# Splitting a second layer's weights in every second step of the first layer, over 16 steps

## The reference

```python
x = x + attention_1(layernorm(x), ctx)     # one head of 512, context of 8 x 120 rows, softmax(q k^T) v
x = x + int8_product(layernorm(x), rhs)    # rows and columns scaled to +-127, rounded, multiplied, scaled back
x = x + attention_2(layernorm(x), ctx)     # 16 heads of 32, weights w_q, w_k, w_v, w_o
x = x + experts(layernorm(x))              # 8 routed experts with capacity 640, one shared expert
```

## Time and profile before

| | before |
|---|---|
| median of the runs | 1309.65 us (1308.88 to 1310.9) |
| the profiled execution | 1312.34 us |
| its span, first to last instruction | 1310.6 us |
| busy in the span: PE, VectorE (DVE), ScalarE (ACT), GpSimd (POOL) | 1238.8, 784.9, 681.1, 574.5 us |
| mean granted TensorE clock | 0.984 |

### The profile page before, as it was taken

One profiled execution on the slowest core, in us unless ns is written; L12 is line 12 of the kernel. 1 busy time (PEld: TensorE's weight loads), 2 busy tenths in 40 slices (PEclk: granted clock), 3 DMA queues, 4 the chain that ended last, 5 costly groups with the idle time before them and its releaser, 6 DMA issues. The chain is left out here.

```text
span 1310.6 us, 27659 instructions
## 1 busy us (share of the span) xinstructions
PE 1238.8 (95%) x10196; PEld 777.5 (59%) x10196; DVE 784.9 (60%) x1615; ACT 681.1 (52%) x1931; POOL 574.5 (44%) x685
## 2 busy tenths in 40 slices
PE   6889998799999999996999999999999999999994
PEld 3556665588888888873444444444444444666762
DVE  5899898799999999893766612121212132544440
ACT  4377777799999999882442111111111121555551
POOL 0056667655666566643000377775002000356533
PEclk9999998999999999998999999999999999899998
DMA  9511023134344434437410402030207000688835
GB/s 347 186 65 66 2 31 44 50 110 142 114 138 138 138 120 134 135 111 161 26 33 1 97 1 65 2 65 2 65 1 241 1 33 9 203 166 221 165 50 71
DMA packets 115445, 122.90 MB, mean 94 GB/s; under 512 B 52816, under 2 KB 77552, under 8 KB 115312
## 3 DMA queue, kind: packets, MB, share of 16 engines
q1 hardware_dynamic: 97472, 98.67, 25.8%
q0 software_dynamic: 13248, 21.15, 8.7%
q10 hardware_dynamic: 4592, 1.32, 0.5%
HBM read 72.35 MB, written 48.80 MB: 92 GB/s over the span
## 5 line engine op out<-in xcount | busy, mean ns | idle before, releaser
L1921 DVE SCALAR_TENSOR_TENSOR shared_hf<-shared_ps_u,shared_sg 128x512 f32<-128x512 f32 x64 | 44.2, 691 | 275.1 <-PE shared_ps_u L111 260.7
L1648 POOL DMA_INDIRECT lists<-shared_load,shared_index x128 | 126.6, 989 | 166.9 <-DVE shared_sk L1789 125.5
L1322 ACT ACTIVATE att_early<-bank,att_early 128x120 f32<-128x120 f32 x512 | 178.9, 377 | 14.1 <-DVE att_early L1190 14.0
L111 PE MATMUL shared_ps_g<-program_xs,program_wgu 128*128 128x512 f16 x768 | 178.4, 382 | 3.5 <-PEq L103 3.5
L1960 PE MATMUL shared_ps_y<-shared_wd,shared_hid 128*128 128x512 f16 x768 | 176.1, 379 | 1.7 <-DVE program_res L1947 1.7
L111 PE MATMUL shared_ps_u<-program_xs,program_wgu 128*128 128x512 f16 x768 | 176.2, 379 | 0.0
L1890 ACT ACTIVATE shared_sg<-shared_ps_g 128x512 f32<-128x512 f32 x64 | 38.2, 597 | 215.3 <-PE shared_ps_g L111 215.3
L1810 POOL DMA_INDIRECT program_x<-xn_rows,program_ex_slots x40 | 38.5, 963 | 243.6 <-PE experts_ps_x L2172 148.4
L111 PEld LDWEIGHTS shared_ps_g<-program_xs,program_wgu 128*128 128x128 f16 x768 | 75.6, 99 | 95.3 <-issue 6.3
L1960 PEld LDWEIGHTS shared_ps_y<-shared_wd,shared_hid 128*128 128x128 f16 x768 | 75.1, 98 | 92.6 <-DVE program_res L1947 2.2
L111 PEld LDWEIGHTS shared_ps_u<-program_xs,program_wgu 128*128 128x128 f16 x768 | 75.1, 98 | 90.7 <-issue 0.2
(11 more groups left out here) (292 smaller groups left out, 2465.5 us busy)
## 6 DMA issues: line engine op xcount, KB each, us to landing
att_place<-q_rows SPq DMA_DIRECT2D x96, 128.0 KB, 2.6
xn_rows<-att_late SPq DMA_DIRECT2D x37, 256.0 KB, 3.1
q_rows<-att_early SPq DMA_DIRECT2D x32, 256.0 KB, 2.1
xt_tiles<-att_late SPq DMA_DIRECT2D x32, 256.0 KB, 2.0
out_rows<-program_res SPq DMA_DIRECT2D x32, 256.0 KB
program_xs<-xt_tiles SPq DMA_DIRECT2D x28, 256.0 KB, 5.1
program_x<-in_x SPq DMA_DIRECT2D x6, 1024.0 KB, 5.4
att_qr<-in_sh_guT SPq DMA_DIRECT2D x8, 512.0 KB, 4.6
```

Source lines behind the costliest of these rows:

```text
L111: last = pe.matmul(out, lhs(a, k), rhs(b, k), start=n == 0, stop=n == len(terms) - 1)
L1322: last = act.activation(prob[:, c, h, :], ps_s[c % 2][:, h, :], ACT.Exp, bias=nmax[:, u % 2, c, h:h + 1], accum_out=rsum[:, u % 2, n:n + 1])
L1648: pool.indirect_dma_start(out=io["lists"], out_offset=bass.IndirectOffsetOnAxis(ap=index[:, t, k:k + 1], axis=0), in_=load[:, t, k, :], in ...
L1921: dve.scalar_tensor_tensor(hf[:, c % 2], ps_u[c % 2][:, :], HS / WS, sg[:, c % 2], ALU.mult, ALU.mult).then_inc(s["hf"], 1)
```

## The change

Before, the eight calls of `split` follow one another in eight steps: ScalarE's in steps 2 to 9, VectorE's in steps 3 to 10. After, there is one in every second step: ScalarE's in steps 2, 4, ... 16, VectorE's in steps 3, 5, ... 17. The order of the weights, the calls themselves and every wait stay.

```diff
     SPLITS = ["L0_Wv", "L1_wvT", "L1_wkT", "L1_wqT", "L1_woT"]
+
+    SPLIT_AT = {2: ("L1_wvT", 0), 4: ("L1_wvT", 1), 6: ("L1_wkT", 0), 8: ("L1_wkT", 1),
+                10: ("L1_wqT", 0), 12: ("L1_wqT", 1), 14: ("L1_woT", 0), 16: ("L1_woT", 1)}
...
             if t == -5:
                 for k in range(KC):
                     quantised(k)
-            if 2 <= t < 10:
-                split(("L1_wvT", "L1_wkT", "L1_wqT", "L1_woT")[(t - 2) // 2], t % 2)
+            if t in SPLIT_AT:
+                split(*SPLIT_AT[t])
...
             if t == -2:
                 columns_out()
-            if 3 <= t < 11:
-                split(("L1_wvT", "L1_wkT", "L1_wqT", "L1_woT")[(t - 3) // 2], (t + 1) % 2)
+            if t - 1 in SPLIT_AT:
+                split(*SPLIT_AT[t - 1])
```

## The result

The changed kernel takes 1315.74 us (median of 19 runs, 1312.0 to 1319.37). The kernel before, run beside it, takes 1311.25 us (19 runs, 1308.31 to 1316.34); the three runs shown first had a median of 1309.65. The ratio is 1.0024, with a 95% interval of 1.0012 to 1.0035: slower by about 3.1 us, between 1.6 and 4.6. (The two medians lie 4.5 us apart, near the upper end of that interval.) The profiled span went from 1310.6 to 1314.5, by 3.9.

The account below looks back on a forecast made before the run. VectorE was taken to set the pace of the front layers until step 11, PE from there. A gain of 3.1 us in steps 4 to 10 and a cost of 5.4 in steps 11 to 17 gave +2.2, 1311.9 us; range 1308.3 to 1313.6.

Parts of the forecast that it names:

- O(18): Start of step 18's weighted-sum matmuls on PE, from which a step is counted; forecast 2.2 us later than before.
- Step 8 goes to 5.73 if VectorE allows: Step 8, losing its VectorE split, falls to PE's 5.73 us, with L685 in the split's place; gain 1.12.
- Step 10 (6.89) likewise: Step 10, also without its VectorE split, falls from 6.89 to 5.73 us; gain 1.16.
- slower: Rival: VectorE still last in steps 8 and 10 through L685 behind L437; up to 2.3 us, 1314.2; chance 0.17.
- so step 11 is priced like 13: Step 11: step 10's ScalarE split falls behind L506, so it takes 7.07 instead of 5.73 us, 1.34 lost.
- Steps 4 to 7: First region: step 4's change gains 0.28 us, step 6 gains 0.57, step 7 keeps its split and about 6.86.
- The odd steps 13, 15, 17: Second region: late ScalarE split and VectorE's split waiting for L437 make each 7.07 instead of 5.73 us; 1.34 lost.
- the bound that I gave for a split that gets in first: Odd late steps: if VectorE's split starts before L437, PE follows at 6.19 us, loss 0.46 a step.
- The even steps 12 to 16: Second region, steps without a VectorE split: 1.05 us of VectorE idle time, nothing further lost or recovered, 5.73 each.
- SyncE's reloads: Four reloads of x, after steps 5, 9, 13, 17, each first read four steps later; cost nothing.
- Shorter stalls: Rival: split beats L437 (forecast to lose by 0.28) or costs a flat 1.56 us; 1308.3 to 1310.1; chance 0.17.
- Faster: Rival: VectorE's 1.05 us idle time and PE's distance to L731 hide the late splits whole; 1306.5; chance 0.06.

Follow-up runs that it names:

- e2: Changed kernel with ScalarE's high part of the v0 jobs in steps 7 to 10 moved ahead of `integers`; 1468.96 us, one run (kernel before 1468.88, other chip).
- e1: Changed kernel with only VectorE's splits spread, ScalarE's back in steps 2 to 9; 1471.02 us, one run (kernel before 1468.88, other chip).
- e3: Changed kernel with GpSimd's second residual cut to one column for tiles 5, 7, 9, 11; 1466.27 us, one run (kernel before 1468.88, other chip).
- e6: Changed kernel with the late splits moved to idle places inside the same steps; 0.9999 of the kernel before (0.9983 to 1.0015).
- e4: Control: kernel before with the same early ScalarE high part as e2; 1470.97 us, one run (kernel before 1468.88, other chip).
- e5: Changed kernel with the edits of e1 and e2 together; 0.9995 of the kernel before (0.9981 to 1.0008).
- e7: wvT and wkT splits as before, wqT and woT one per step in e6's places, plus e2's early high part; 0.9979 of the kernel before (0.9965 to 0.9992).

## Why the prediction was right or wrong

**The time.** Forecast: 1311.9, +2.2, no change that could be told. Measured: +3.1 by the ratio, 1315.74 by the median, above the range's 1313.6. Of the 3.8 us between 1311.9 and 1315.74, 1.6 are the reference itself (1311.25 in the longer series against 1309.65), 1.1 are the step below, as O(18) shows, and 1.1 are not located: the medians lie 4.5 us apart where the traces' first layers lose 3.3. The step below alone would have given 1313.0, inside the range. The side was the forecast's, toward slower; its size went past the 0.2% mark (2.6 us): 2.2 us lie under it, the traces' 3.3 above.

**The step that failed: "Step 8 goes to 5.73 if VectorE allows ... gain 1.12. Step 10 (6.89) likewise: gain 1.16."** Measured gains: 0.14 and 0.13. I let L685 take the split's place at O + 4.36 and asked only whether GpSimd would be in its way. Its input from ScalarE, which comes at O + 5.73, I didn't look up; in the trace of before that wait didn't show because the split stood in front of it. e2 shows it: with that one instruction earlier, the two steps take 5.73 and 5.78. The rival "slower" had the right place and the right price (VectorE still last in steps 8 and 10, up to 2.3 us; it was 2.0) but the wrong cause, the meeting with GpSimd, which e2 measures at what the sum had for it, with PE still last in step 8.

**Step 11: "so step 11 is priced like 13".** It lost 0.51, not 1.34, only because step 10 was still late: ScalarE found its job early and its split was hidden. In e2 the step takes 6.99. This is the same error's other side; together: 0.98 + 1.03 - 0.83 for steps 8, 10 and 11 and -0.09 for the others is +1.1, from the forecast's 2.2 to the measured 3.3. That the two sums lie so near owes something to luck: at O(11) the gain is 1.13 instead of 3.13, and the cost behind it 4.46 instead of 5.36; the first error brought the second with it, and the second cancels part of the first.

**What held.** Steps 4 to 7 (O(6) earlier by 0.27 and O(7) by 0.84; VectorE's freed time in step 4 went to a wait of 0.81 at 78.95 for ScalarE, whose split stood in front). The odd steps 13, 15, 17: 7.03 to 7.04 for 7.07, with each part seen: ScalarE's lateness (e1: 0.79 of it), the split's wait for the residual (e3: 6.18 or 6.19 without it, the bound that I gave for a split that gets in first). The even steps 12 to 16. SyncE's reloads: nobody waited for a tile, and VectorE has no idle time before L697's counterpart. The granted clock is 1.00 in every stretch of steps 7 to 14 shown.

**The rivals.** "Shorter stalls": the split lost the race in steps 13, 15 and 17, by 0.29, 0.30 and 0.29, so the margin of 0.28 held. "Faster": not with a split in front of L731; but e6 shows that the 1 us of idle time does hide it if it stands in the idle time itself, which is not what the change did.

## What to carry to other kernels

Before an instruction is taken out of a full engine, look up every input of the one that moves up into its place: a wait that the removed one covered doesn't show in the trace. An instruction moved into another step brings its place in that step along: at the end of the step it stood in front of what the bounding engine waits for, and beside a GpSimd instruction that shuts it out; in the idle time before the next wait the same instruction was free. And an engine with time to spare still makes others late if the added work stands ahead of what they wait for.

## What the runs showed of the hardware that was not expected

Where a VectorE instruction with two SBUF inputs meets GpSimd's residual, the rest of the residual is added to that instruction's length, less about 0.13 us. A split lasted 1.21 alone (e3), 1.56 when the residual had 0.48 left (e1: residual 130.31 to 131.58, split at 131.10), 2.06 when it had 0.98 left; in both meetings VectorE went on 1.01 after the residual's end. e2's low part fits as well: 0.68 alone, 1.10 with 0.54 left. In the other direction GpSimd's one-column L435 took 1.17 behind a split, and 0.19 or 0.20 without one. VectorE's L745, with one input, took its usual 0.68 beside the same residual (e1, 130.51). The Trainium skill, SBUF — State Buffer, section "Who interferes with whom", calls this an exclusive lock; the traces agree, and with the 0.13, read from these runs, such lengths can be forecast in this kernel.

One step of the hand-over between the layers, step 30, lies far from the change and is the same program in all nine traces, and yet its length differs by up to 2.9 us, together with the granted clock. The kernel before had TensorE at half its full clock, at the 1.2 GHz level, there (stretches of the kernel before, columns as in the earlier trace rows):

```profile
215.00:219.00 4.00, 1.72 (x20) 1.24 (x17) 3.97 (x11) 2.60 (x7) 3.86 (x6) 0.93 0.16 28
219.00:222.40 3.40, 3.03 (x8) 1.27 (x9) 2.41 (x9) 2.59 (x4) 1.92 (x5) 0.50 0.00 0
222.40:225.80 3.40, 3.40 (x33) 3.19 (x32) 2.97 (x9) 0.95 (x3) 2.59 (x5) 0.57 0.02 5
```

and e3 did not:

```profile
215.00:219.00 4.00, 2.14 (x22) 1.52 (x20) 4.00 (x8) 3.02 (x7) 3.86 (x6) 1.00 0.20 35
219.00:222.40 3.40, 2.55 (x23) 1.81 (x24) 3.37 (x11) 2.49 (x4) 2.45 (x5) 1.00 0.00 0
222.40:225.80 3.40, 3.40 (x56) 3.35 (x55) 3.37 (x10) 2.34 (x6) 2.69 (x5) 1.00 0.02 5
```

In both PE had been waiting in the 4 us ahead of it (busy 1.72 and 2.14 us). Step 30 starts at O(30), 219.37 in the kernel before. It takes 8.70 in the kernel before, 8.78 in the changed one and 8.72 in e4; 7.3 to 7.5 in e2, e5, e6 and e7, where the clock was back at 1.00 earlier; and 5.88 in e3 and 5.86 in e1, where it never fell. What decides between these isn't known, and no run changes the clock alone. Both kernels' profiled executions had the long form, so their spans compare like with like. The scatter between runs goes with the clock too: of the changed kernel's 19 runs, the eight with a mean clock of 0.987 or 0.988 have spans of 1310.3 to 1313.0 us (median 1311.6), the eleven with 0.983 to 0.986 have 1312.8 to 1317.7 (median 1314.4). That this one step makes the difference isn't shown.
